# Another opening order, zeros written in 39 pieces, later q/k transposes and 42 matmuls of constants in a transformer layer

## The chip, the cores and the metric

One core of one Trainium2 chip runs the whole program. The metric is the device time of one execution in microseconds; the median of three executions of the kernel before is 1262.27 us.

## What is computed

One post-norm transformer layer over 2048 tokens of width 512. Of the reference, cut down:

```
qkv = x @ w_qkv                                  # 16 heads of 32
q, k = unit_norm(q), unit_norm(k)                # t * rsqrt(sum(t*t) + 1e-6)
q, k = rope on the even heads, unchanged on the odd ones
attn = softmax(causal(q @ k.T * q_gain))
x = layernorm(x + (attn @ v) @ w_out)
x = layernorm(x + routed_ffn(x) + shared_ffn(x)) # 8 experts, top 2, hidden 352; shared 704
```

## The kernel before

**Precision.** A product of float32 operands is made of three: each operand is split into a rounded high part and a low part, and high*high, low*high and high*low add up in PSUM. So each x tile is transposed by TensorE (PE), its high half is copied out by ScalarE (ACT, `xT_h`) and its low half by VectorE (DVE, `xT_l`).

**Attention.** Heads go in four groups of four (`g`), tokens in four chunks of 512 (`c`), 16 tiles of 128. For each group: 16 projections (`pe_project`, 12 matmuls of 384 columns, one tile each), whose q and k part ACT copies to `qk_even` or `qk_odd` and whose squares it writes to `squares`; `dve_norms` per chunk (a reduction, a chain of small operations, one large product, then the rotation of q, while GpSimd (POOL) rotates k); then q and k are turned (`pe_turn`, four transposes into `turn_ps`), split (`act_turn_high`, `dve_turn_low`), stored to DRAM and loaded again into `q_stack` and `k_stack` in another layout by the queue of SP (`stack`: two stores, a wait for both to land, three loads). Only then can the scores of that chunk begin.

**Slots.** A group's scores are 40 slots. Chunk 0 has slots 0 to 3, chunk 1 slots 4 to 11, chunk 2 slots 12 to 23, chunk 3 slots 24 to 39. In a slot PE makes the scores of one key tile, then whatever the tables put there, then the products with v of the slot before (`pe_values`); ACT takes the exponentials; the softmax sums are either matmuls on PE (slots in `DIRECT`) or additions on DVE (three heads) and POOL (one head), `key_sum`, which `pe_sums` gathers at the end of a chunk. Tables written by hand (`PROJECT_AT`, `NORMALISE_AT`, `TURN_AT`) say in which slot the projection, normalisation and turns stand; chunks 0 and 1 of the next group are prepared in slots 25 to 39 of this one. Each engine runs its own list strictly in this order, so what stands behind a waiting instruction waits too. Group 0 is written out, groups 1 and 2 are a loop, group 3 is written out again.

**Opening.** x comes through four buffers, so that a load waits for the transposes of the tile four before. All 16 tiles are transposed, chunks 0 and 1 of group 0 are projected, and one DMA writes 39 tiles of zeros (9984 KB) to `x_sorted`, which the expert stage needs much later.

**After attention** come the output projection, the router, the shared FFN and 39 expert tiles; the change touches there only the semaphore count that the scatter waits for.

Of the kernel before, what the change touches and what calls it, by code (L numbers as in the profile page):

```python
# [65 lines left out]
                (1, 0): 36, (1, 1): 37}  # L66
TURN_AT = {(2, 0): 8, (2, 1): 9,
           (3, 0): 15, (3, 1): 16,
           (0, 0): 31, (0, 1): 32,
           (1, 0): 38, (1, 1): 39}  # L70
# [8 lines left out]
NORM_AFTER = 7  # L79

FIRST_AFTER = 5
# [6 lines left out]
def work_at(table, slot, g):  # L88

    if table is TURN_AT and isinstance(g, int) and g == 0 and slot == 0:  # L90
        for which in range(2):
            yield 0, 1, which
# [12 lines left out]
def build(nc, x, w_qkv, w_out, q_gain, gate_w, w_gate, w_up, w_down, sw_gate, sw_up, sw_down,  # L105
          rope_cos, rope_sin, numbers, out):
    with ExitStack() as ctx:
# [21 lines left out]
        x_in = at("x_in", 135168, [P, 4, D], F32)  # L129
# [4 lines left out]
        squares = at("squares", 180224, [P, 2, TPC, HG, HD], F32)  # L134
        rope_prod = at("rope_prod", 180224, [P, 2, 4, TPC, HG // 2, HD // 2], F32)
# [35 lines left out]
        x_loaded = [sem(f"x_loaded{n}") for n in range(4)]  # L171
# [91 lines left out]
        zeros = at("zeros", 159744, [P, D], F32)  # L263
# [717 lines left out]
        def tail_gpsimd(pool):  # L981
# [11 lines left out]
            pool.wait_ge(zero_filled, 16)  # L993
# [54 lines left out]

        def load_w(sp, g):
# [6 lines left out]
        def _(sp):  # L1056
            for t in range(NT):
                if t >= 4:
                    sp.wait_ge(x_turned, t - 3)
                sp.dma_start(x_in[:, t % 4, :], x_rows[t * P:(t + 1) * P, :]).then_inc(x_loaded[t % 4], 16)  # L1060
                if t == 3:
                    load_w(sp, 0)
                    sp.dma_start(tile_numbers[:], numbers.rearrange("(a h) -> a h", a=1).broadcast_to([P, MAX_TILES])).then_inc(numbers_loaded, 16)
                    for to, of in ((cos, rope_cos), (sin, rope_sin)):
                        for c in range(NC):
                            sp.dma_start(to[:, c], of[c * CH:(c + 1) * CH, :].rearrange("(t p) f -> p t f", p=P)).then_inc(tables_loaded, 16)
                    sp.dma_start(gain[:], q_gain.rearrange("(a h) -> a h", a=1).broadcast_to([P, HEADS])).then_inc(tables_loaded, 16)
# [55 lines left out]
        def pe_project(g, c, tt):  # L1123
# [28 lines left out]
        def pe_scores(g, slot):  # L1152
# [7 lines left out]
            for p in range(2):  # L1160
                if later(g) or slot:
                    nc.tensor.wait_ge(exp_done, 2 * n + p - 1)
                for hh in range(2):
# [41 lines left out]
        def _(pe):  # L1205
            pe.wait_ge(consts_ready, 1)
            for t in range(NT):
                pe.wait_ge(x_loaded[t % 4], 16 * (t // 4 + 1))
                if t >= 4:
                    pe.wait_ge(xT_low, t - 3)  # L1210
                for k in range(KC):
                    mm = nc.tensor.transpose(scores[:, (t % 4) // 2, t % 2, k * P:(k + 1) * P],
                                             x_in[:, t % 4, k * P:(k + 1) * P], ident[:])
                mm.then_inc(x_turned, 1)
                if 0 <= t - FIRST_AFTER < TPC:

                    pe.wait_ge(xT_low, TPC)
                    pe.wait_ge(xT_high, TPC)
                    pe.wait_ge(ident_ready, 1)
                    pe_project(0, 0, t - FIRST_AFTER)  # L1220
            pe.wait_ge(xT_low, NT)
            pe.wait_ge(xT_high, NT)
            for which in range(2):
                pe_turn(0, 0, which)
            for tt in range(TPC):
                pe_project(0, 1, tt)
            def group(g):
                for slot in range(SLOTS):
# [3 lines left out]
                    for work in work_at(TURN_AT, slot, g):  # L1232
                        pe_turn(*work)
                    if slot or later(g):
# [5 lines left out]


        def act_copy_qkv(g, c, tt):
# [10 lines left out]
            if tt == 0 and (later(g) or c):  # L1253
                nc.scalar.wait_ge(q_roped, 2 * C)
                nc.scalar.wait_ge(k_roped, 2 * C)
            nc.scalar.activation(squares[:, :, tt], rows, ACT.Square)
# [296 lines left out]
```

## Time and profile before

| | us |
|---|---|
| median of 3 executions | 1262.27 (1262.16 to 1262.39) |
| the profiled execution | 1263.19 |
| its span | 1261.4 |
| TensorE busy in it | 1127.5 |

The sum of the prediction is made against the profiled execution's 1263.19 us, of which 1261.4 us are the span from the first to the last instruction and 1.8 us lie around it. Attention ends near 660 us of the span.

### The profile page before, as it was taken

What the parts mean: (1) busy time and instruction counts of PE and PEld (TensorE: products, weight loads), DVE (VectorE), ACT (ScalarE), POOL (GpSimd) and SP (SyncE); (2) the same over time, 40 slices, a digit from 0 to 9 for tenths busy, and PEclk for the clock granted to TensorE, in tenths of its full rate; (3) what the DMA queues carried; (4) which work ended last, traced back from release to release, by engine and by line L of the source; (5) the groups of instructions that cost most, each with busy time, mean ns of one, the idle gap of its engine ahead of it and who ended that gap; (6) DMA issues with size and microseconds to landing.
All of it is one profiled execution on the core that took longest, in us unless ns stands there. A gap on an engine that the chain in (4) does not pass through costs nothing.

```text
span 1261.4 us, 19831 instructions
## 1 busy us (share of the span) xinstructions
PE 1127.5 (89%) x6618; PEld 798.4 (63%) x6619; DVE 610.3 (48%) x1120; ACT 544.4 (43%) x894; POOL 499.9 (40%) x360
## 2 busy tenths in 40 slices
PE   5459899998979989998989999598999999999984
PEld 5446355654545545564337887367899999997763
DVE  2424876368553675645845846122222222222774
ACT  3226775566655666656852541011222332321131
POOL 1002555046340463422863206725246464622530
PEclk9869999999999999999988999789999999999997
DMA  5952502334131341324406302833244453412341
GB/s 144 367 148 70 139 11 84 101 84 117 51 101 44 84 125 43 101 59 125 144 1 207 117 1 85 310 105 92 95 143 153 135 166 127 146 59 76 107 160 67
DMA packets 90621, 141.73 MB, mean 112 GB/s; under 512 B 12272, under 2 KB 36848, under 8 KB 90544
## 3 DMA queue, kind: packets, MB, share of 16 engines
q1 hardware_dynamic: 74320, 103.48, 27.1%
q10 hardware_dynamic: 10944, 19.93, 4.6%
q0 software_dynamic: 5280, 17.31, 4.2%
q8 instruction: 47, 0.77, 0.3%
q14 instruction: 30, 0.25, 0.1%
HBM read 84.59 MB, written 56.10 MB: 112 GB/s over the span
## 4 chain that ended last, share of the span: by engine, by line
PE 64%; DVE 16%; issue 8%; POOL 4%; ACT 3%; DMA 2%; SPq 1%; another core or an unknown queue 1%; ACTq 0%; DVEq 0%; POOLq 0%
PE scores L497 12%; PE bank L1134 9%; PE scores L1166 7%; PE bank L490 7%; PE scores L554 5%; PE bank L1191 5%; PE bank L585 5%; PE scores L414 3%; PE bank L1188 3%; POOL key_sum L1493 3%; ACT probs L1292 2%; PE scores L512 1%; DVE key_sum L1407 1%; DVE x L861 1%; DMA turn_scratch<-turned_l 1%
## 5 line engine op out<-in xcount | busy, mean ns | idle before, releaser
L1292 ACT ACTIVATE probs<-scores,shift_now 128x1024 f32<-128x1024 f32 (+3 forms) x320 | 299.3, 985 | 132.8 <-PE scores L1166 62.5
L1166 PE MATMUL scores<-q_stack,k_stack 96*128 96x512 f32 (+3 forms) x640 | 205.7, 425 | 22.3 <-DMA k_stack<-turn_scratch 13.8
L1166 PEld LDWEIGHTS scores<-q_stack,k_stack 96*128 96x128 f32 x640 | 116.0, 198 | 155.3 <-issue 74.8
L1493 POOL TENSOR_TENSOR key_sum<-key_sum,probs 128x512 f32<-128x512 f32 (+2 forms) x76 | 154.4, 2031 | 128.1 <-ACT probs L1292 124.4
L1407 DVE TENSOR_TENSOR key_sum<-key_sum,probs 128x1536 f32<-128x1536 f32 (+2 forms) x76 | 157.0, 2066 | 42.7 <-ACT probs L1292 40.8
L1191 PE MATMUL bank<-probs,v_sb 128*32 128x512 f32 (+3 forms) x1280 | 152.4, 548 | 0.0
L497 PE MATMUL scores<-ffn_w,xt_h 128*128 x624 | 131.9, 334 | 4.6 <-issue 4.5
L964 POOL TENSOR_TENSOR ffn_w<-raw,ones 128x1408 fp32r<-128x1408 f32 (+2 forms) x36 | 71.6, 2000 | 150.7 <-PE bank L490 103.3
L554 PE MATMUL scores<-x1T_h,ffn_w 128*128 128x512 f32 (+1 forms) x384 | 104.2, 403 | 11.3 <-issue 8.9
L497 PEld LDWEIGHTS scores<-ffn_w,xt_h 128*128 128x128 f32 x624 | 103.4, 190 | 13.7 <-issue 11.7
L554 PEld LDWEIGHTS scores<-x1T_h,ffn_w 128*128 128x128 f32 (+1 forms) x384 | 69.1, 182 | 37.2 <-issue 13.5
L968 POOL TENSOR_TENSOR ffn_w<-raw,ffn_w 128x1408 fp32r<-128x1408 f32 (+2 forms) x36 | 90.6, 2527 | 2.1
L775 DVE TENSOR_TENSOR ht_l<-scores,ht_h 128x256 fp32r<-128x256 f32 x39 | 16.6, 425 | 146.7 <-ACT ht_h L649 146.7
L690 ACT CAST hid_h<-silu 128x512 fp32r<-128x512 f32 (+1 forms) x24 | 14.9, 620 | 149.9 <-DVE silu L806 130.6
L1381 POOL TENSOR_TENSOR rope_prod<-qk_even,cos 128x128 f32<-128x128 f32 x8 | 4.5, 564 | 187.5 <-DVE qk_even L1370 187.5
L490 PE MATMUL bank<-ffn_w,ht_h 128*128 (+1 forms) x234 | 70.4, 409 | 0.0
L1134 PE MATMUL bank<-wqkv_h,xT_h 128*128 128x384 f32 x256 | 60.3, 358 | 7.1 <-ACT v_sb L1260 7.1
L1191 PEld LDWEIGHTS bank<-probs,v_sb 128*32 128x32 f32 x1280 | 33.3, 111 | 50.6 <-issue 46.1
L1021 POOL DMA_INDIRECT extra<-y_sorted,place_int x32 | 35.3, 1102 | 71.7 <-DVE x L861 33.5
L497 PE MATMUL scores<-ffn_w,xt_l 128*128 x312 | 63.5, 325 | 0.0
L1188 PE MATMUL bank<-probs,ones 128*32 128x512 f32 (+3 forms) x576 | 62.7, 507 | 0.2
L585 PE MATMUL bank<-ffn_w,hid_h 128*128 128x512 f32 (+1 forms) x192 | 54.6, 413 | 8.6 <-ACT hid_h L690 7.1
(207 smaller groups left out, 1835.5 us busy)
## 6 DMA issues: line engine op xcount, KB each, us to landing
q_stack<-turn_scratch SPq DMA_DIRECT2D x48, 256.0 KB, 3.9
k_stack<-turn_scratch SPq DMA_DIRECT2D x48, 256.0 KB, 3.9
x_sorted<-zeros SPq DMA_DIRECT2D x1, 9984.0 KB, 28.9
y_sorted<-y_tile ACTq DMA_DIRECT2D x39, 256.0 KB, 2.2
x_tile<-x_sorted ACTq DMA_DIRECT2D x37, 256.0 KB, 2.7
turn_scratch<-turned_h SPq DMA_DIRECT2D x32, 256.0 KB, 2.9
turn_scratch<-turned_l SPq DMA_DIRECT2D x32, 256.0 KB, 3.1
raw<-w_gate SPq DMA_DIRECT2D x8, 704.0 KB
```

Of the source, the lines that this page charges most:

```text
L490: mm = nc.tensor.matmul(out_tile[:], hs[0:kn, k, :], moving(slot_before, DOWN + (low * 3 + k) * D, D, kn), start=(m == 0 and k == 0), stop ...
L497: mm = nc.tensor.matmul(to[:, 0:FH], xs[:, k, :], moving(slot, first + (low * KC + k) * FH, FH), start=(m == 0 and k == 0), stop=(m == 2 a ...
L554: mm = nc.tensor.matmul(scores[0:hn, which, n % 2, :], stationary(slot, at_, low, k, h0, hn), xs[:, k, c * CH:(c + 1) * CH], start=(m == 0 ...
L585: mm = nc.tensor.matmul(bank[n % 2][:], hs[0:kn, k, tt * P:(tt + 1) * P], ffn_w[0:kn, slot, first:first + D], start=(m == 0 and k == 0), s ...
L968: last = nc.gpsimd.tensor_tensor(low, src, high.bitcast(F32), ALU.subtract)
L1134: mm = nc.tensor.matmul(qkv_ps[:, 0:3 * P], xs[:, k, tok], ws[:, k, :], start=(m == 0 and k == 0), stop=(m == 2 and k == KC - 1))
L1166: mm = nc.tensor.matmul(scores[:, p, hh, lo:CH], k_stack[0:3 * HD, h, j * P:(j + 1) * P], q_stack[0:3 * HD, i % 2, h, lo:CH], start=True, ...
L1188: nc.tensor.matmul(sums_ps[HD * h:HD * (h + 1), lo:CH], ones[:], probs[:, slot % 4, h, lo:CH], start=first, stop=(j == last))
L1191: mm = nc.tensor.matmul(y_ps[HD * h:HD * (h + 1), lo:CH], v_sb[:, j, HD * h:HD * (h + 1)], probs[:, slot % 4, h, lo:CH], start=(j == 0), s ...
L1292: nc.scalar.activation(probs[:, slot % 4, 2 * p:2 * p + 2, lo:CH], scores[:, p, :, lo:CH], ACT.Exp, bias=shift_now[:, p:p + 1]).then_inc(e ...
L1407: nc.vector.tensor_tensor(key_sum[:, 0:3, lo:CH], key_sum[:, 0:3, lo:CH], probs[:, slot % 4, 0:3, lo:CH], ALU.add).then_inc(sum_dve, 1)
L1493: nc.gpsimd.tensor_tensor(key_sum[:, 3, lo:CH], key_sum[:, 3, lo:CH], new, ALU.add).then_inc(sum_pool, 1)
```

## The change

It has six parts. (1) x gets a buffer for each tile (`x_early` for 12, `x_late` for 4), SP issues all loads at once, w_qkv right after the first tile, the rope tables as two DMAs at the end. (2) The opening runs in the order of `OPENING`, the first projection right behind the first tile; DVE splits w after tile 0, and POOL's half of that split no longer waits for the tables. Tiles 12 to 15 are transposed in slots 4 to 6 of group 0, through the one bank `turn_ps`. (3) The zeros come from a source of 128x128, as 39 DMAs of 256 KB, 13 in each of groups 0 to 2. (4) `TURN_AT` is later everywhere: chunk 1's turns go to slots 0 and 2 of the group that uses them (in group 0: 2 and 3), chunk 0's from slots 31 and 32 to 33 and 36. The projections of chunk 1 go to slots 31 to 34, its normalisation to 35. (5) `DIRECT` loses slots 14, 15, 28, 29 and gains 13, 22. (6) 14 and 28 matmuls of bf16 ones stand ahead of and behind the first tile's transposes.

```
-              (1, 0): 32, (1, 1): 32, (1, 2): 34, (1, 3): 35}
+              (1, 0): 31, (1, 1): 32, (1, 2): 33, (1, 3): 34}
-                (1, 0): 36, (1, 1): 37}
-TURN_AT = {(2, 0): 8, (2, 1): 9,
+                (1, 0): 35, (1, 1): 36}
+TURN_AT = {(1, 0): 0, (1, 1): 2,
...
-DIRECT = set(range(STEP_AT[1])) | {4, 5, 6, 10, 11, 14, 15, 23, 28, 29, 30, 36, 38, 39}
+DIRECT = set(range(STEP_AT[1])) | {4, 5, 6, 10, 11, 13, 22, 23, 30, 36, 38, 39}
...
+FIRST_TURN_AT = (2, 3)
+EARLY = 3 * TPC
+LATE_X_AT = {4: [12], 5: [13, 14], 6: [15]}
+OPENING = [("x", 0), ("p", 0), ("x", 1), ("x", 2), ("p", 1), ("x", 3), ("x", 4), ("p", 2), ("x", 5), ("x", 6),
+           ("p", 3), ("x", 7), ("x", 8), ("p", 4), ("x", 9), ("p", 5), ("x", 10), ("p", 6), ("t", 0), ("t", 1),
+           ("x", 11), ("p", 7)]
+IDLE_MATMULS = (14, 28)
+FILL_AT = [4, 5, 6, 7, 11, 14, 15, 16, 25, 26, 27, 28, 29]
...
+                    if g < NG - 1 and slot in FILL_AT:
+                        sp.wait_ge(scores_ready, 2 * (SLOTS * g + slot))
+                        fill_zeros(len(FILL_AT) * g + FILL_AT.index(slot))
...
-                        sp.wait_ge(turned, 2 * (4 * g + 4))
+                        sp.wait_ge(turned, 2 * (NC * g + 3))
+                        sp.wait_ge(q_roped, 2 * (NC * g + 4))
+                        sp.wait_ge(k_roped, 2 * (NC * g + 4))
...
+        def pe_warm(count):
+            for _ in range(count):
+                nc.tensor.matmul(sums_ps[:, 0:P], ones_b[:], ones_b[:], start=True, stop=True)
...
+        def pe_turn_x(t):
+            nc.tensor.wait_ge(x_loaded[t], 16)
+            if t == EARLY:
+                nc.tensor.wait_ge(turn_low, 4)
+            elif t > EARLY:
+                nc.tensor.wait_ge(xT_low, t)
...
```

PE's list at the start of the program. Before, six x tiles (24 transposes) stand ahead of the first projection:

```order
L1212 MATMUL scores<-ident,x_in 128x128 x24
L1134 MATMUL bank<-wqkv_h,xT_h 128x384 x4
L1134 MATMUL bank<-wqkv_h,xT_l 128x384 x4
L1134 MATMUL bank<-wqkv_l,xT_h 128x384 x4
L1212 MATMUL scores<-ident,x_in 128x128 x4
```

And of the change, the same place:

```order
L1166 MATMUL bank<-ones_b 128x128 x14
L1178 MATMUL scores<-ident,x_early 128x128 x4
L1166 MATMUL bank<-ones_b 128x128 x28
L1159 MATMUL bank<-wqkv_h,xT_h 128x384 x4
L1159 MATMUL bank<-wqkv_h,xT_l 128x384 x4
L1159 MATMUL bank<-wqkv_l,xT_h 128x384 x4
L1178 MATMUL scores<-ident,x_early 128x128 x8
```

One tile stands ahead of the first projection, two behind it, and the constants' matmuls around the tile.

DVE's list at the end of group 0, slots 36 to 39 before (from the large product of chunk 1's normalisation on; `key_sum` 3x384 is slot 37, `turned_l` x2 are chunk 1's halves of slots 38 and 39):

```order
L1370 TENSOR_TENSOR qk_odd<-qk_odd,inv_norm 128x1024
L1381 TENSOR_TENSOR rope_prod<-qk_odd,cos 128x128
L1382 TENSOR_TENSOR rope_prod<-qk_odd,sin 128x128
L1383 TENSOR_TENSOR rope_prod<-qk_odd,sin 128x128
L1384 TENSOR_TENSOR rope_prod<-qk_odd,cos 128x128
L1386 TENSOR_TENSOR qk_odd<-rope_prod 128x8x16
L1387 TENSOR_TENSOR qk_odd<-rope_prod 128x8x16
L1407 TENSOR_TENSOR key_sum<-key_sum,probs 128x3x384
L1392 TENSOR_TENSOR turned_l<-bank,turned_h 128x512 x2
```

And of the change, slots 35 to 39, from the same product on:

```order
L1424 TENSOR_TENSOR qk_odd<-qk_odd,inv_norm 128x1024
L1435 TENSOR_TENSOR rope_prod<-qk_odd,cos 128x128
L1436 TENSOR_TENSOR rope_prod<-qk_odd,sin 128x128
L1437 TENSOR_TENSOR rope_prod<-qk_odd,sin 128x128
L1438 TENSOR_TENSOR rope_prod<-qk_odd,cos 128x128
L1440 TENSOR_TENSOR qk_odd<-rope_prod 128x8x16
L1441 TENSOR_TENSOR qk_odd<-rope_prod 128x8x16
L1446 TENSOR_TENSOR turned_l<-bank,turned_h 128x512
L1461 TENSOR_TENSOR key_sum<-key_sum,probs 128x3x384
```

The `turned_l` here is k of chunk 0 of the next group, turned in slot 36; before, it stood ahead of this normalisation (slot 32), and now it stands behind it.

PE's list around slots 4 to 6 of group 0 in the change (late x tiles into a bank that is not of `scores`):

```order
L1178 MATMUL bank<-ident,x_late 128x128 x4
L1235 MATMUL bank<-probs,ones 32x128 x4
L1238 MATMUL bank<-probs,v_sb 32x128 x4
L1213 MATMUL scores<-q_stack,k_stack 128x512 x4
L1178 MATMUL bank<-ident,x_late 128x128 x8
L1235 MATMUL bank<-probs,ones 32x512 x4
L1238 MATMUL bank<-probs,v_sb 32x512 x4
```

Two tiles (x8) stand in one slot, ahead of that slot's products with v; before, the slots held only scores and these products.

## Rows read from the trace of the kernel before

**Rows 1.** The page: busy us by engine; ACT's exponentials (busy, mean ns | idle before, releaser).
```profile
PE 1127.5 (89%) x6618; PEld 798.4 (63%) x6619; DVE 610.3 (48%) x1120; ACT 544.4 (43%) x894; POOL 499.9 (40%) x360
...
L1292 ACT ACTIVATE probs<-scores,shift_now 128x1024 f32<-128x1024 f32 (+3 forms) x320 | 299.3, 985 | 132.8 <-PE scores L1166 62.5
```

**Rows 2.** Timeline of the opening: start, duration in us, engine, line, operation [idle before <-releaser].
```profile
9.19 0.96 DVE L1333 CAST wqkv_h<-wqkv_raw 128x1536 fp32r<-128x1536 f32 x1 [0.18 <-DMA wqkv_raw<-w_qkv]
...
11.12 20.43 SPq L1060 DMA_DIRECT2D x_in<-x  x12
13.98 3.44 POOL L1475 TENSOR_TENSOR wqkv_l<-wqkv_raw,wqkv_h 128x1536 fp32r<-128x1536 f32 x1 [10.74 <-DMA gain<-q_gain]
14.91 1.97 PE L1212 MATMUL scores<-ident,x_in 128*128 128x128 f32 x8 [7.24 <-DMA x_in<-x]
...
22.96 0.60 PE L1212 MATMUL scores<-ident,x_in 128*128 128x128 f32 x4
...
30.68 1.22 DVE L1358 TENSOR_REDUCE sq_sum<-squares 128x32 f32<-128x1024 f32 x1 [4.58 <-ACT v_sb L1260]
31.59 0.43 SPq L1070 DMA_DIRECT2D x_sorted<-zeros  x1
...
38.15 0.28 DVE L1387 TENSOR_TENSOR qk_even<-rope_prod 128x128 f32<-128x128 f32 x1
...
42.74 0.59 ACT L1299 CAST xT_h<-scores 128x512 fp32r<-128x512 f32 x1
```

**Rows 3.** Chain that ended last, opening to the first scores: start, us, what.
```profile
24.12 2.34 PE bank L1134 x12
...
52.40 9.38 DMA turn_scratch<-turned_l
...
61.80 0.32 SPq L1089
...
74.07 0.76 PE scores L1166
```

**Rows 4.** DMA issues of the page: tensors, queue, count, KB each, us to landing.
```profile
x_sorted<-zeros SPq DMA_DIRECT2D x1, 9984.0 KB, 28.9
```

**Rows 5.** Windows, TensorE alone, start of group 2: stretch, its length, busy (x), PEclk, DMA share, GB/s.
```profile
374.00:382.00 8.00, 3.92 (x16) 0.50 0.53 156
```

**Rows 6.** The chain, slots 4 to 7 of group 0.
```profile
95.83 1.13 PE scores L1166 x4
...
100.78 0.99 PE bank L1188 x8
...
105.69 1.12 PE scores L1166 x4
```

**Rows 7.** The chain of group 1, and the start of group 2.
```profile
225.06 0.43 PE scores L1166
...
273.11 1.23 DVE sq_sum L1358
...
287.64 0.69 DVE turned_l L1392
...
292.41 0.68 PE scores L1166 x2
...
310.92 3.48 POOL wqkv_l L1475
...
359.27 1.22 DVE sq_sum L1358
...
369.18 0.65 DVE turned_l L1392
...
372.00 2.93 DMA q_stack<-turn_scratch
374.97 0.79 PE scores L1166
```

**Rows 8.** Waits of TensorE, whole attention: who for whom, us in total, times, longest.
```profile
PE bank L1148 <- DVE qk_odd L1387: 10.2, 7, 1.9
```

More of the change, by code:

```diff
@@ L88, in work_at @@
 def work_at(table, slot, g):
-    if table is TURN_AT and isinstance(g, int) and g == 0 and slot == 0:
-        for which in range(2):
-            yield 0, 1, which
+    if table is TURN_AT and isinstance(g, int) and g == 0 and slot < TPC:
+        if slot in FIRST_TURN_AT:
+            yield 0, 1, FIRST_TURN_AT.index(slot)
+        return
     for (c, part), at in table.items():
@@ L170, in build @@
         shift_steps, shift_copied = sem("shift_steps"), sem("shift_copied")
[L171 removed]
+        x_loaded = [sem(f"x_loaded{n}") for n in range(NT)]
         x_turned, xT_high, xT_low = sem("x_turned"), sem("xT_high"), sem("xT_low")
@@ L1136, in pe_project @@
             mm.then_inc(qkv_done, 1)
+        def pe_warm(count):
[7 more added lines that the diff above has]
+                nc.tensor.wait_ge(xT_low, t)
+            elif t >= 4:
+                nc.tensor.wait_ge(xT_low, t - 3)
+            for k in range(KC):
+                mm = nc.tensor.transpose(xT_bank(t)[:, k * P:(k + 1) * P], x_tile_in(t)[:, k * P:(k + 1) * P], ident[:])
+            mm.then_inc(x_turned, 1)
         def pe_turn(g, c, which):
             C = NC * g + c
+            if not later(g) and c == 2:
+                nc.tensor.wait_ge(xT_low, NT)
             if which == 0:
@@ L1205, in _ @@
         def _(pe):
+            pe.wait_ge(mask_filled, 1)
+            pe_warm(IDLE_MATMULS[0])
             pe.wait_ge(consts_ready, 1)
[L1207 to L1226, printed above, removed]
+            for kind, n in OPENING:
+                if (kind, n) == ("p", 0):
+                    pe_warm(IDLE_MATMULS[1])
+                if kind == "x":
+                    pe_turn_x(n)
+                elif kind == "p":
+                    pe_project(0, n // TPC, n % TPC)
+                else:
+                    pe_turn(0, 0, n)
             def group(g):
@@ L1233, in group @@
                         pe_turn(*work)
+                    if not later(g):
+                        for t in LATE_X_AT.get(slot, []):
+                            pe_turn_x(t)
                     if slot or later(g):
@@ L1239, in _, with squares_of, act_x_high @@
             tail_tensor(pe)
+        def squares_of(g, c):
+            return squares_second if not later(g) and c == 1 else squares
+        def act_x_high(t):
+            nc.scalar.wait_ge(x_turned, t + 1)
+            nc.scalar.copy(xT_h[:, :, t * P:(t + 1) * P], xT_bank(t).rearrange("p (k n) -> p k n", k=KC)).then_inc(xT_high, 1)
         def act_copy_qkv(g, c, tt):
@@ L1252, in act_copy_qkv @@
             nc.scalar.copy(qk[c % 2][:, :, tt], rows)
-            if tt == 0 and (later(g) or c):
+            if tt == 0 and (later(g) or c >= 2):
                 nc.scalar.wait_ge(q_roped, 2 * C)
                 nc.scalar.wait_ge(k_roped, 2 * C)
-            nc.scalar.activation(squares[:, :, tt], rows, ACT.Square)
+            nc.scalar.activation(squares_of(g, c)[:, :, tt], rows, ACT.Square)
             if later(g):
@@ L1279, in act_exp @@
             lo = max(0, (j - TPC * i) * P)
-            if not later(g) and slot == 3:
-                nc.scalar.wait_ge(zero_filled, 16)
             if not later(g) and slot == 0:
-                nc.scalar.wait_ge(x_turned, NT)
+                nc.scalar.wait_ge(x_turned, EARLY)
             if later(g) or slot >= 4:
@@ L1322, in group @@
                         act_turn_high(*work)
+                    if not later(g):
+                        for t in LATE_X_AT.get(slot, []):
+                            act_x_high(t)
             each_group(act, group)
@@ L1450, in _ @@
-            for which in range(2):
-                dve_turn_low(0, 0, which)
+            for t in range(8):
+                dve_x_low(t)
+                if t == 0:
+                    dve_split_w(0)
+            dve.wait_ge(tables_loaded, 16 * (3))
+            nc.vector.tensor_scalar(gain_abs[:], gain[:], -1.0, None, ALU.mult).then_inc(shift_steps, 1)
+            dve.wait_ge(shift_steps, 1)
+            nc.vector.tensor_tensor(gain_abs[:], gain_abs[:], gain[:], ALU.max).then_inc(shift_steps, 1)
@@ L1452, in _ @@
+            dve_norms(0, 0)
+            for t in range(8, EARLY):
+                dve_x_low(t)
+                if EARLY - 3 <= t < EARLY - 1:
+                    dve_turn_low(0, 0, t - EARLY + 3)
             dve_norms(0, 1)
@@ L1456, in group @@
                         dve_turn_low(*work)
+                    if not later(g):
+                        for t in LATE_X_AT.get(slot, []):
+                            dve_x_low(t)
                     if slot in STEP_AT and (slot or later(g)):
@@ L1486, in pool_add_keys @@
                 nc.gpsimd.wait_ge(sum_pool, added(g, slot) - 1)
+            if not later(g) and slot == first_added(ADDING[0]):
+                nc.gpsimd.wait_ge(x_turned, NT)
             if slot == first_added(i) and (later(g) or i > ADDING[0]):
```

105 lines of the change are left out of this document (53 added, 52 removed).

## Prediction

> **What bounds the kernel now.** I read the page first: TensorE (PE) is busy for 1127.5 of 1261.4 us [rows 1], so it is the engine to follow, and only stretches in which it waits, or does work that can go, are worth anything. Then the timeline of the opening: SP's loads of x are issued only from 11.12 us on; PE's next transposes begin at 14.91 after 7.24 us of waiting for x; POOL's half of the w split begins at 13.98, after the last table. The reader should see that DVE's first normalisation starts at 30.68 and that the DMA of zeros is issued at 31.59, just ahead of the first q/k stores [rows 2]. The chain shows what that does: the low half's store takes 9.38 us to land, the q loads start at 61.80, and the first scores come at 74.07 [rows 3]. From there I read the chain slot by slot in group 0 [rows 6] and group 1 [rows 7]: PE paces most slots, and hands over to DVE or POOL behind each normalisation and at the w split. The windows show a third limit: after a wait the clock stands at 1.2 GHz (PEclk 0.50) for 8 us and more, in which PE gets less done [rows 5].
>
> **The opening: 21 us gained.** w is now second in the queue instead of fifth and waits for no table. Four tiles and w, 1.8 MB, were in at 9.19 [rows 2], some 7 us after the first data; tile 0 and w are 1.05 MB, so my estimate is 6.5 us. DVE then rounds it (1 us), POOL subtracts (3.44 us [rows 2]): both halves by 11.0. The first projection ends at 11.8. The next must wait for ACT's copies (1.0) and for two halves of tile 1 (0.6 and 0.7): it ends at 16.8. After that a cycle is two tiles' transposes (0.60 each [rows 2]) and a projection (2.34 [rows 3]), about 3.65 us with the wait: the fourth ends at 24.1. DVE's tile 7 is out at 26.6, five small operations follow, and the normalisation starts at 27.7 against 30.68: only 3 us of the 6 saved on w arrive here, since a cycle now holds two tiles of x, and the normalisation stands behind tile 7. It takes 7.7 us as before (30.68 to 38.43 [rows 2]) and ends at 35.4. Then x tiles 8 and 9 and the q half on DVE, until 37.5; its store lands near 41 with nothing before it, where the wait lasted until 61.80. From the first q load to the first scores it was 12.3 us (61.80 to 74.07 [rows 3]): now 53.3. The gain is 21 us. If the tables, now last in the queue, come late or the landings are slow, 15; if the k half overlaps better, 24.
>
> The 42 constants' matmuls cost nothing by this: 28 of them at 0.11 to 0.15 us (a 128x128 transpose, four in 0.60 [rows 2]) are 3 to 4.2 us, from 4.8 to 9 at the latest, under the wait for w's low half at 11.0. Without that cover they would cost up to 4 us. They may keep the clock up for the first projection, which is also hidden.
>
> **Group 0, slots 0 to 7: 9 us lost.** Before, slot 4 began 21.8 us after slot 0 (95.83 less 74.07 [rows 3, 6]). Chunk 1's turns leave slot 0, but q is now turned in slot 2, 14.4 us in, and needs ACT and DVE (1.4), a store (3), three loads (1.3) and their landing (3 to 4): ready 23.5 to 24.5 us in. PE would be there at 20.3. So slot 4 comes about 2 us later than before relative to slot 0. In slots 4 to 6, the single bank makes the late x tiles a ping-pong: tile 13 waits for tile 12's two halves, which on ACT stand behind the exponentials, a copy of y and the copies of a projection; tile 14 in the same slot waits for two exponentials (0.985 each by the mean [rows 1], 1.06 of this width), ACT's 0.59 [rows 2] and DVE's 0.7 of tile 13. PE, counted through, reaches slot 7 16.5 us after slot 4 instead of 9.9 (95.83 to 105.69 [rows 6]): 1.8 us are the four tiles' transposes, 4.9 the two waits. Together 9 us; bounds 5 (q arrives in time, one wait hidden) and 13 (the clock falls as well).
>
> **Slots 8 to 25, each group: 2.7 us gained.** All times from here are on group 1's clock of the trace, as if its slot 0 began where it did. Today k and q of chunk 3 are turned in slots 15 and 16, where PE waits for the normalisation of 273.11 and then for DVE's half at 287.64, so that slot 17 starts only at 292.41 [rows 7]. With q at slot 18 and k at 22 these waits go. But slot 13 is now a direct one, the first to use the sums bank, and DVE reads the old sums only behind the normalisation, at 283.9; PE waits there for 2.5 us instead. Counting ACT's two exponentials a slot (2.1 us) and 2.4 us for an addition on DVE or POOL from there, slot 24 begins 3.8 us earlier. The w load now comes after q's stack in slot 18, some 3 us later than before, so w's low half, at 310.92 + 3.48 [rows 7], moves only to 311.8, and 2.7 us are left.
>
> **Slots 26 to 39 and the next group's start.** Two direct slots less are 2 x 0.99 us of PE (one direct slot's sums [rows 6]), the late turns take away PE's waits for q in slots 31 and 38 (seven such waits for the odd chunks alone are 10.2 us, the longest 1.9 [rows 8]); PE is done at 363.5 instead of just before 372.00 [rows 7]. But the scores of the next group need k of chunk 0, and its low half now stands on DVE behind chunk 1's normalisation. That begins at 356.8 (before 359.27 [rows 7]), takes 8.2 us, and the half is out at 365.7. From there to q's loads it was 2.2 us and their landing 2.93 (369.83, 372.00 [rows 7]); with three issues 6.5: scores at 372.2. So PE waits 8.7 us, and most of what it saved is given back. Against 374.97 [rows 7] this is 2.8 us better in group 1, whose end had a stall at the loop's turn already; groups 0 and 2 have none there, and for them the same sum gives 0.5 and 0.9 us. Moreover such a wait is as long as the one that brought the clock to 1.2 GHz before slot 0 of group 2 (0.50 from 374 to 382 [rows 5]); that costs slots 0 and 1 about 3 us in groups 1 and 3, while group 2 may even gain 1. Group 3 has no next group and keeps 2.5 of its gain: behind the w_out split POOL's two more additions take the rest.
>
> The 39 pieces of zeros: 9984 KB took 28.9 us [rows 4], so 0.74 us each, and they are spread over slots without a stack beside them; SP issues one in 0.43 [rows 2]. I count nothing. A piece that runs into a stack's store delays it by 0.74 at most, and PE only in slot 4 and at a group's end, where none stands. Beside it, the Trainium skill (DMA: Bandwidth & Descriptors, Rules for kernel authors) asks for at least 1 MiB a transfer, which speaks against the pieces; no trace here shows a 256 KB one of zeros, and rival (c) is what it would come to if they didn't hide.
>
> **Sum:** -21 + 9 - 0.5 - 2.8 - 0.9 - 2.5 + 6 - 1 = -13.7. The profiled execution would go from 1263.2 to 1249.5, the median, 0.9 lower today, to 1248.5.
>
> **Rivals.** (a) *The boundary's wait is shorter*: the normalisation starts or the landing ends 3 us sooner than counted at each of three boundaries, and the clock falls at one of them less: -9 and -3, 1236.5. For it: the start at 356.8 is counted through ten slots. Against it: k's half stands behind the normalisation in DVE's list. 0.25. (b) *The opening gives less*: x, which is issued at once, and 64-byte table pieces fill the queue, so that the first normalisation stays near 30.7; then only the zeros' removal counts, 15 us, and slots 4 to 6 cost 13: 1258. 0.14. (c) *Slower than before*: the zeros' pieces do not hide. SP's queue is one, and every store and load of a stack stands behind the pieces; 13.7/39 = 0.35 us of PE for each of the 39 would use up the gain; at 0.74 each it is -13.7 + 28.9 = +15.2, 1277.5. It decides from 0.35 us a piece on. Speaking for it: the 9.38 us landing beside the zeros [rows 3]. Against it: that was behind 10 MB, not 256 KB, and the slots were chosen between stacks. 0.06. (d) *The change does little*: the opening's gain is all taken back at boundaries at half clock (10 instead of 3 us each): within 2.5 us of 1262. 0.05.
>
> **How the numbers follow.** My forecast has 0.50: 1243 to 1255. The range reaches over (a) and (b): 1236 to 1259. A measurement of this kernel tells 0.2%, 2.5 us. Faster by more 0.92, the same 0.03, slower 0.05.
>
> **What would show it.** First scores at 53 us (51 to 59); POOL's split of w done by 11; the first normalisation at 27.7; slot 4 to slot 7 of group 0 16.5 us; PE waiting for k_stack's DMA before slot 0 of groups 1 to 3 for over 5 us, with PEclk 0.50; slots 15 and 16 without waits for turns. The prediction is wrong if PE runs through the group's boundary, or if the first normalisation doesn't move.

## The result and the profile after

The changed kernel is slower. Its median is 1268.9 us (1267.5 to 1269.7, four executions) against 1262.2 us of the kernel before, measured beside it; the ratio is 1.0051 with a 95% interval of 1.0032 to 1.0069. The forecast was 1248.5 us. The profiled execution took 1268.5 us, 5.3 more than that of before.

The page of the changed kernel: its span, and busy time by engine.

```profile
span 1266.6 us, 19869 instructions
...
PE 1129.4 (89%) x6596; PEld 804.2 (63%) x6597; DVE 623.7 (49%) x1128; ACT 541.2 (43%) x894; POOL 540.5 (43%) x368
```

TensorE has 22 instructions less than before, 64 of its sums matmuls having gone and 42 of constants come, and is busy 1.9 us longer [rows 1]. POOL is busy 40.6 us more with 8 instructions more. Both are signs to follow: matmuls at a lower clock, and work that got slower beside other work.

The chain of the changed kernel from the first load to the first scores: start, us, what.

```profile
2.27 5.12 DMA wqkv_raw<-w_qkv
...
8.46 3.46 POOL wqkv_l L1529
...
36.73 2.02 DMA turn_scratch<-turned_l
38.77 0.32 SPq L1106
...
50.72 0.77 PE scores L1213
```

The opening did what it should. The low half's store lands after 2.02 us where it took 9.38, and the scores come 23.35 us earlier than at 74.07 [rows 3]. So the loss lies behind 50.72, and there it is 28.6 us. To find it, the span is cut where a slot's first scores matmul starts. The table is worked out from those starts in the trace (us, rounded; "24 to 32" includes slot 32; the columns from the third on are sums over the groups named):

| kernel | to first scores | g0 slots 0 to 7 | g1 to g3 slots 0 to 7 | all slots 8 to 23 | g0 to g2 slots 24 to 32 | g0 to g2 slot 33 to next group | g3 slots 24 to 39 | rest |
|---|---|---|---|---|---|---|---|---|
| before | 74.1 | 36.6 | 102.1 | 200.4 | 120.8 | 77.4 | 45.0 | 604.9 |
| after | 50.7 | 47.4 | 107.2 | 199.2 | 121.7 | 88.6 | 45.6 | 606.2 |
| e1, whole loop as before | 51.5 | 47.4 | 98.9 | 200.6 | 121.9 | 74.1 | 45.3 | 602.8 |
| e12, only DIRECT new | 50.2 | 47.6 | 99.0 | 200.4 | 136.1 | 76.8 | 46.3 | 605.5 |
| e7, only DIRECT old | 51.8 | 47.2 | 106.7 | 190.2 | 109.6 | 89.2 | 44.9 | 605.5 |
| e9, 28 and 29 direct again | 52.2 | 47.1 | 107.0 | 194.2 | 107.4 | 89.2 | 43.6 | 608.0 |
| e3, k half in slot 34 | 50.5 | 48.9 | 104.8 | 198.9 | 122.6 | 66.6 | 46.8 | 602.9 |
| e10, e7 and e3 together | 50.6 | 47.4 | 105.2 | 187.7 | 109.3 | 66.7 | 44.1 | 604.9 |
| e11, e10 with both x edits | 52.1 | 35.0 | 104.9 | 188.1 | 109.7 | 66.9 | 43.6 | 608.3 |

Against before, the changed kernel loses 10.7 in group 0's slots 0 to 7, 5.2 in the others', and 11.2 from slot 33 to the next group. What should have paid for it, the slots 8 to 32, gives 0.4. The waits say where TensorE stands now. The view of waits, changed kernel: who for whom, us in total, times, longest.

```profile
PE scores L1213 <- DMA k_stack<-turn_scratch: 16.8, 2, 8.7
PE bank L1159 <- ACT v_sb L1309: 14.4, 5, 4.6
PE bank L1235 <- DVE inv_sum L1470: 11.7, 4, 3.0
...
PE bank L1178 <- DVE xT_l L1380: 3.5, 2, 1.9
```

Each line is one place. The first is the group's boundary, the second slot 32, the third slot 14 (four groups, 3 us each), the last the late x tiles. The view puts the third boundary's 8.2 us down to "issue" instead of k. The boundary's wait stood in the forecast at its size, slot 14's at 2.5, the late x waits at 4.9 in all; the wait in slot 32 did not stand there.

**Slot 14.** The timeline of group 1 around it, rows of DVE and PE: start, duration, engine, line, operation [idle before].

```profile
273.67 1.22 DVE L1424 TENSOR_TENSOR qk_odd<-qk_odd,inv_norm 128x1024 f32<-128x1024 f32 x1
...
277.18 0.70 DVE L1470 STREAM_TRANSPOSE inv_sum<-bank 128x512 f32<-128x512 f32 x1
...
278.03 1.93 PE L1235 MATMUL bank<-probs,ones 128*32 128x512 f32 x8 [2.96 <-DVE inv_sum L1470]
...
279.71 1.96 PE L1238 MATMUL bank<-probs,v_sb 128*32 128x512 f32 x8
...
281.60 2.08 PE L1213 MATMUL scores<-q_stack,k_stack 96*128 96x512 f32 x4
```

The windows of the same place, TensorE alone: stretch, length, busy (x), PEclk, DMA share, GB/s.

```profile
274.00:278.00 4.00, 1.07 (x4) 0.85 0.00 0
278.00:282.00 4.00, 3.97 (x17) 0.50 0.35 125
```

Slot 13 is a direct one now, its sums go to the bank that DVE still has to read, and DVE reads it only behind the normalisation. TensorE waits 2.96 us, and then sums, products and scores run at half clock (0.50 in the window 278.00:282.00), 1.93, 1.96 and 2.08 us, where at full clock they are 1.07, 1.07 and 1.20 (e7's rows below). The wait was forecast at 2.5; that the work behind it doubles was not.

**Slot 32.** The timeline of group 1, slots 29 to 32, DVE, POOL, ACT and PE:

```profile
326.22 1.76 DVE L1461 TENSOR_TENSOR key_sum<-key_sum,probs 128x1536 f32<-128x1536 f32 x1 [2.48 <-ACT probs L1341]
327.90 1.21 DVE L1412 TENSOR_REDUCE sq_sum<-squares 128x32 f32<-128x1024 f32 x1
...
336.01 1.97 POOL L1441 TENSOR_TENSOR qk_even<-rope_prod 128x128 f32<-128x128 f32 x1
...
338.07 0.38 ACT L1305 ACTIVATE squares<-bank 128x256 f32<-128x256 f32 x1 [6.53 <-POOL qk_even L1441]
...
338.66 1.65 PE L1159 MATMUL bank<-wqkv_h,xT_h 128*128 128x384 f32 x4 [4.55 <-ACT v_sb L1309]
340.11 1.48 PE L1159 MATMUL bank<-wqkv_h,xT_l 128*128 128x384 f32 x4
```

The addition of slot 29 stands on DVE ahead of chunk 0's normalisation and waits for that slot's exponentials. So the reduction starts at 327.90, the rotation of k ends on POOL at 337.98, and only then may ACT write `squares` of chunk 1's first projection (both use the same memory). The last product of that rotation took 1.97 us here, beside DVE's next addition, and 0.45 in e9 below. TensorE, which needs the projection's bank again, waits 4.55 us, and again works at half clock behind it: 1.65 and 1.48 us for four matmuls that take 0.86 to 0.97 at full clock.

**The boundary.** The chain from group 1 to group 2:

```profile
356.88 1.22 DVE sq_sum L1412
...
364.56 0.69 DVE turned_l L1446
365.26 2.04 DMA turn_scratch<-turned_l
...
368.21 4.74 DMA k_stack<-turn_scratch
...
373.19 0.79 PE scores L1213
```

This is the forecast's chain, link for link: the low half of k behind the normalisation, two landings, scores. A trap lies in it: the normalisation was forecast at 356.8 "on group 1's clock of the trace" and starts at 356.88, but group 1 itself began at 217.7 and not 225.06 [rows 7]. Within the group it is 7.4 us late. The windows behind the three boundaries:

```profile
217.00:225.00 8.00, 7.29 (x47) 0.68 0.00 0
373.00:381.00 8.00, 7.81 (x46) 0.61 0.00 0
528.00:536.00 8.00, 7.25 (x39) 0.50 0.01 2
```

Each group now starts below full clock; before, groups 1 and 3 started at 1.00 (windows 225.00:233.00 and 528.00:536.00) and only group 2 at 0.50 [rows 5].

### The profile page after: what moved, and what is told of

Its sections match the earlier page's. It is cut to its first block, busy times and chain, and to the rows that moved or that the text cites. A ratio compares the mean times of both kernels' runs of the same rounds, so it can differ in the third digit from the quotient of the medians.

```text
span 1266.6 us, 19869 instructions
## 1 busy us (share of the span) xinstructions
PE 1129.4 (89%) x6596; PEld 804.2 (63%) x6597; DVE 623.7 (49%) x1128; ACT 541.2 (43%) x894; POOL 540.5 (43%) x368
## 4 chain that ended last, share of the span: by engine, by line
PE 66%; DVE 13%; issue 8%; POOL 5%; ACT 3%; DMA 2%; another core or an unknown queue 1%; SPq 0%; ACTq 0%; POOLq 0%; DVEq 0%
PE scores L505 12%; PE bank L1159 10%; PE scores L1213 9%; PE bank L1238 7%; PE bank L498 6%; PE scores L562 6%; PE bank L593 5%; PE scores L422 3%; PE bank L1235 3%; ACT probs L1341 2%; POOL key_sum L1549 2%; DVE x L869 2%; PE scores L520 1%; PE scores L1216 1%
## 5 line engine op out<-in xcount | busy, mean ns | idle before, releaser
L1213 PE MATMUL scores<-q_stack,k_stack 96*128 96x512 f32 (+3 forms) x640 | 208.6, 429 | 48.0 <-issue 18.9
L1549 POOL TENSOR_TENSOR key_sum<-key_sum,probs 128x512 f32<-128x512 f32 (+1 forms) x84 | 190.5, 2268 | 88.6 <-ACT probs L1341 84.2
L1461 DVE TENSOR_TENSOR key_sum<-key_sum,probs 128x1536 f32<-128x1536 f32 (+1 forms) x84 | 179.5, 2137 | 68.9 <-ACT probs L1341 66.9
L1446 DVE TENSOR_TENSOR turned_l<-bank,turned_h 128x512 fp32r<-128x512 f32 x32 | 21.9, 686 | 110.0 <-ACT turned_h L1316 109.9
L1235 PE MATMUL bank<-probs,ones 128*32 128x512 f32 (+3 forms) x512 | 53.9, 495 | 11.7 <-DVE inv_sum L1470 11.7
L1238 PEld LDWEIGHTS bank<-probs,v_sb 128*32 128x32 f32 x1280 | 32.8, 112 | 47.6 <-issue 41.2
```

The lines of the kernel that those rows point to most:

```text
L1213: mm = nc.tensor.matmul(scores[:, p, hh, lo:CH], k_stack[0:3 * HD, h, j * P:(j + 1) * P], q_stack[0:3 * HD, i % 2, h, lo:CH], start=True, ...
L1235: nc.tensor.matmul(sums_ps[HD * h:HD * (h + 1), lo:CH], ones[:], probs[:, slot % 4, h, lo:CH], start=first, stop=(j == last))
L1238: mm = nc.tensor.matmul(y_ps[HD * h:HD * (h + 1), lo:CH], v_sb[:, j, HD * h:HD * (h + 1)], probs[:, slot % 4, h, lo:CH], start=(j == 0), s ...
L1461: nc.vector.tensor_tensor(key_sum[:, 0:3, lo:CH], key_sum[:, 0:3, lo:CH], probs[:, slot % 4, 0:3, lo:CH], ALU.add).then_inc(sum_dve, 1)
L1549: nc.gpsimd.tensor_tensor(key_sum[:, 3, lo:CH], key_sum[:, 3, lo:CH], new, ALU.add).then_inc(sum_pool, 1)
```

## The experiments

All kernels have one of two bases, named with each. Ratios are against the kernel before, run beside them. Its medians were 1262.2 us beside the changed kernel, 1266.0 beside e1 to e4, 1263.5 beside e5 to e8 and 1265.6 beside e9 to e12, so a difference between kernels of two of these series is uncertain by some 4 us. Theory 1 is the one of the forecast's own parts (each part costs what its place shows, and they add up); the rival is in each expectation.

**e1: the whole loop as before, everything else new.**

```
-              (1, 0): 31, (1, 1): 32, (1, 2): 33, (1, 3): 34}
+              (1, 0): 32, (1, 1): 32, (1, 2): 34, (1, 3): 35}
...
-DIRECT = set(range(STEP_AT[1])) | {4, 5, 6, 10, 11, 13, 22, 23, 30, 36, 38, 39}
+DIRECT = set(range(STEP_AT[1])) | {4, 5, 6, 10, 11, 14, 15, 23, 28, 29, 30, 36, 38, 39}
```

(The other two tables likewise.)

> The change with the projection, normalisation and turn tables and the direct slots of before; opening order, late x tiles, chunk 1's first turns in slots 2 and 3, zeros in 39 pieces and the constants' matmuls stay. By stages of the trace of the change, the opening gains 23.4 us and slots 0 to 8 of group 0 lose 10.8. Theory 1 (the later turns and the other direct slots lose the rest, mostly at the groups' boundaries): all groups take from slot 8 on what they took before, so about 1262.2 - 23.4 + 10.8 = 1249.6, within 2. Rival 2 (the 39 pieces of zeros slow the groups they lie in, whatever the tables): groups 0 to 2 stay longer and the time is 1258 to 1268.

Measured: 1245.5 us, ratio 0.986 (0.980 to 0.991). That is 2 us below the range of theory 1 and far from the rival. The new opening, group 0's late x tiles included, is good for about 20 us, and the new loop takes 23 away.

**e2: the kernel before with the new tables and the new DIRECT** (and the waits of SP and the turns of group 0's chunk 1 that the new tables need).

> The kernel before with only the new tables, the new direct slots and the w load's waits that go with them; opening, x buffers and the single zeros DMA of before. Theory 1: it is slower by what the groups lost from slot 8 of group 0 on, 16 to 19 us: 1278 to 1281, with TensorE waiting for k_stack before slot 0 of groups 1 to 3. Rival 2 (the zeros' pieces are what slows the groups): 1260 to 1266.

Measured: 1282.1 us, ratio 1.012 (1.009 to 1.015), 1 us above theory 1's range. The loss is the loop's own; it needs neither the early opening nor the zeros' pieces. Its table, cut the same way, has 107.1 us in groups 1 to 3's slots 0 to 7, 122.8 in the slots 24 to 32 and 88.8 from slot 33 on, as the changed kernel.

**e3: the k half of chunk 0 turned two slots earlier.**

```
-           (0, 0): 33, (0, 1): 36}
+           (0, 0): 33, (0, 1): 34}
```

> The change with one number other: k of chunk 0 of the next group is turned in slot 34 instead of 36, so that its low half stands on VectorE ahead of chunk 1's normalisation, not behind it. Theory 1 (this half behind the normalisation makes TensorE wait 5.6 to 10 us at each of three boundaries, and the clock falls to 1.2 GHz after it): the waits go, 5 us at each boundary and 3 us of slow clock at two of them: 1268.9 - 21 = 1248, at least 12 us less. Rival 3 (what ends last at the boundary is the normalisation of chunk 1 itself, through the additions and the sums of chunk 3): only 0 to 5 us less, 1264 to 1269.

Measured: 1245.5 us, ratio 0.983 (0.980 to 0.986), theory 1. One number gives 23 us. Its slots 33 to the next group are 66.6 us in sum, 10.8 less than even before.

**e4: the four late x tiles turned in the opening.**

```
-LATE_X_AT = {4: [12], 5: [13, 14], 6: [15]}
+LATE_X_AT = {}
...
-           ("x", 11), ("p", 7)]
+           ("x", 11), ("p", 7), ("x", 12), ("x", 13), ("x", 14), ("x", 15)]
```

> The change with x tiles 12 to 15 transposed behind the last projection of the opening, where TensorE waits for the first k anyway, instead of in slots 4 to 6 of group 0. Theory 1 (the single bank's ping-pong and its waits cost 6 to 8 us there, and TensorE's idle stretch before the first scores is free): 1261 to 1263. Rival 4 (VectorE's four halves delay chunk 1's normalisation, so that q comes later to slot 4, and the gain goes): 1266 to 1269.

Measured: 1262.7 us, ratio 0.997 (0.995 to 0.999), theory 1. The slots 4 to 7 of group 0 took 16.4 us and not 24.2, and the first scores still came at 50.2: in the opening the four tiles cost nothing, since TensorE waits there for q's way through DRAM.

**e5: no matmuls of constants.**

```
-IDLE_MATMULS = (14, 28)
+IDLE_MATMULS = (0, 0)
```

> The change without the 42 matmuls of constants. Theory 1 (the first projection waits 1.86 us for w's low half anyway, so neither their time nor the clock they keep up is on the path): the first scores within 1 us of 50.7, the whole within 0.15% of the change (1267 to 1271). Rival 5 (without them the first transposes and projections run at 1.2 GHz): first scores 1.5 to 3 us later, 1270 to 1272.

Measured: 1267.0 us, ratio 1.0020 (1.0000 to 1.0041), whose interval overlaps that of the changed kernel. The timeline shows why; the first projection of e5:

```profile
8.15 1.65 PE L1159 MATMUL bank<-wqkv_h,xT_h 128*128 128x384 f32 x4 [3.53 <-DVE wqkv_h L1387]
...
9.60 1.48 PE L1159 MATMUL bank<-wqkv_h,xT_l 128*128 128x384 f32 x4
11.69 0.97 PE L1159 MATMUL bank<-wqkv_l,xT_h 128*128 128x384 f32 x4 [0.61 <-POOL wqkv_l L1529]
```

Without the constants the first two sets take 1.65 and 1.48 us, as in slot 32 at half clock (the view's clock reads 1.00 here, so this rests on the durations), but they end before POOL's half of w is there. The scores began at 50.5 against 50.7.

**e6: all 39 pieces of zeros issued in the opening,** ahead of the first store, in the slots none.

> The change with all 39 pieces of zeros issued right behind the loads, ahead of the first q/k stores, instead of spread over slots. Theory 1 (the opening's gain is mostly the store of q and k that no longer stands behind 10 MB of zeros): the pieces run from about 20 to 50 us, the low half of q lands near 50 instead of 38.8, first scores at 60 to 63: 10 to 12 us slower than the change, 1279 to 1281. Rival 6 (the gain is the earlier projections; 39 pieces from 20 us on are nearly over when the stores come at 36): first scores at 51 to 54, 1269 to 1272.

Measured: 1291.3 us, ratio 1.021 (1.016 to 1.026), 22 more than the changed kernel and 10 more than expected. The first scores came at 70.1, 19.4 later. SP's queue in e6:

```profile
19.43 34.90 SPq L1085 DMA_DIRECT2D x_sorted<-zeros  x39
54.37 0.86 SPq L1097 DMA_DIRECT2D turn_scratch<-turned_h  x1
```

The pieces went out over 34.90 us, and q's store stands behind them on the same queue; the one large DMA landed in 28.9 [rows 4] after a single issue of 0.43 [rows 2]. In the slots the same pieces cost nothing that shows: the loop of e6, which has none of them, is no shorter than the changed kernel's (613.5 us from the first scores to the last slot of group 3, against 609.7). The Trainium skill (DMA: Bandwidth & Descriptors, Rules for kernel authors), cited in the forecast against pieces below 1 MiB, agrees in direction with e6. That the size is the reason is not shown, since the pieces also come from a narrower source, 512 bytes a row where it had 2048. Spread over the slots it doesn't matter.

**e7: only DIRECT as before** (14, 15, 28, 29 direct, 13 and 22 not).

> The change with the direct slots of before (14, 15, 28, 29 back, 13, 22 out), the later turns kept. Theory 1 (the additions of slots 28 and 29 delay chunk 0's normalisation, by which TensorE waits 4.5 us in slot 32 of groups 0 to 2, and stand behind the w_out split on GpSimd in group 3, 7.5 us instead of 3.2; slot 13 as a direct one costs 2.8 us of waiting in each group): those go and two more direct slots cost 2 us a group, 1256 to 1263. Rival 7 (TensorE's work counts more than these waits): 1269 to 1277.

Measured: 1242.3 us, ratio 0.981 (0.977 to 0.986): 26.6 us less than the changed kernel, where 6 to 13 were expected. It is a cost of the size of the k turn's (which of the two is the larger isn't shown: their intervals overlap), and I had not seen it. The table says where: -9.0 in the slots 8 to 23 and -12.1 in the slots 24 to 32. Slot 14 in e7, DVE and PE:

```profile
273.41 0.70 DVE L1470 STREAM_TRANSPOSE inv_sum<-bank 128x512 f32<-128x512 f32 x1
...
274.26 1.07 PE L1235 MATMUL bank<-probs,ones 128*32 128x512 f32 x8 [1.09 <-DVE inv_sum L1470]
...
275.12 1.07 PE L1238 MATMUL bank<-probs,v_sb 128*32 128x512 f32 x8
...
276.12 1.20 PE L1213 MATMUL scores<-q_stack,k_stack 96*128 96x512 f32 x4
```

The direct slots 14 and 15 come a slot later, the wait is 1.09 and the clock stays up.

**e8: e1 with the late x tiles in the opening and group 0's chunk 1 turned in slots 0 and 1.**

```
-FIRST_TURN_AT = (2, 3)
+FIRST_TURN_AT = (0, 1)
```

> Opening order, zeros in pieces and constants of the change; projection, normalisation and turn tables and direct slots of before; x tiles 12 to 15 transposed in the opening; chunk 1's first turns in slots 0 and 1 of group 0 instead of 2 and 3. Theory 1 (terms add: run e1 less the ping-pong's 7.8 us and the 3 us wait for q in slot 4): 1233 to 1236. Rival 8 (chunk 1's normalisation isn't done by slot 0, so the turns make TensorE wait there): 1238 to 1242.

Measured: 1234.5 us, ratio 0.976 (0.971 to 0.981). The parts of the opening and of group 0 add up: its slots 0 to 7 took 35.0 us, 1.6 less than before.

**e9: slots 28 and 29 direct again, 13 and 22 kept.**

```
-DIRECT = set(range(STEP_AT[1])) | {4, 5, 6, 10, 11, 13, 22, 23, 30, 36, 38, 39}
+DIRECT = set(range(STEP_AT[1])) | {4, 5, 6, 10, 11, 13, 22, 23, 28, 29, 30, 36, 38, 39}
```

> The changed kernel with one edit: the slots 28 and 29 accumulate on TensorE again (DIRECT holds them as before), while 13 and 22 stay in the place of 14 and 15. Theory 1: what DIRECT costs comes for the most part from these two slots, whose additions on GpSimd delay the squares and norm of the next group's chunk 0 behind them. In the kernel with DIRECT as before, slot 32 took 4.2 us and not 10.4 to 11.3, the slots 24 to 31 took 32.0 to 32.7 us and not 29.3 to 29.7, and in the last group 24.7 and not 27.1. That gives -6.8 x 3 + 2.8 x 3 - 2.4 = -14.4, so 1268.9 - 14.4 = about 1254.5 (1252 to 1257), with the slots 8 to 23 still at about 49.6 us a group. Theory 2: the swap of 14 and 15 for 13 and 22 carries the cost: at least 1263, and slot 32 keeps its wait.

Measured: 1249.7 us, ratio 0.988 (0.984 to 0.991): 19.2 us less, theory 1, by more than it said. Slot 29 and 32 of group 1 in e9, DVE, POOL, ACT and PE:

```profile
317.03 1.22 DVE L1412 TENSOR_REDUCE sq_sum<-squares 128x32 f32<-128x1024 f32 x1 [4.13 <-ACT v_sb L1309]
...
325.20 0.45 POOL L1441 TENSOR_TENSOR qk_even<-rope_prod 128x128 f32<-128x128 f32 x1
...
326.14 0.39 ACT L1305 ACTIVATE squares<-bank 128x256 f32<-128x256 f32 x1
...
328.65 0.86 PE L1159 MATMUL bank<-wqkv_h,xT_h 128*128 128x384 f32 x4
```

Slot 29 begins at 316.6 here and at 323.2 in the changed kernel. The reduction starts 0.4 us into it instead of 4.7, the rotation ends before ACT wants the memory, and TensorE doesn't wait; slot 32 took 4.2 us in each group, where it was 10.4 to 11.3. Of e7's 26.6 us, 7.4 are left for the swap of 14 and 15 for 13 and 22.

One part was not in the expectation: in the slots 8 to 23, whose DIRECT e9 shares with the changed kernel, groups 0 to 2 took 48.0, 48.3 and 48.1 us, not 49.6, 50.4 and 49.5. At slot 14 of group 1, e9 waits 2.50 for `inv_sum` and the clock stays at full:

```profile
269.00:273.00 4.00, 1.76 (x12) 1.00 0.00 0
273.00:277.00 4.00, 3.74 (x28) 1.00 0.29 103
```

So the clock after this wait, full here and half in the changed kernel, carries some 1.6 us a group. In group 3 of e9 it fell (wait 2.44), and that group took 49.8 as in the changed kernel (49.7). This gain is not one of the edit for sure: e5 has the changed kernel's tables and DIRECT, and there the clock fell behind slot 14 in two groups and not in four, and the same slots took 195.6 us in sum instead of 199.2. The length of the wait does not settle it either. Slot 14 of group 2 in e4, whose clock fell (0.50 in the window 427.00:430.00), and of group 0 in e9, whose clock stayed:

```profile
426.45 1.86 PE L1231 MATMUL bank<-probs,ones 128*32 128x512 f32 x8 [1.86 <-DVE inv_sum L1466]
124.09 1.06 PE L1235 MATMUL bank<-probs,ones 128*32 128x512 f32 x8 [2.69 <-DVE inv_sum L1470]
```

Over the eight kernels with 13 as a direct slot, the granted clock of the 8 us from these sums on was below 1.00 behind 24 of the 32 waits: behind all 20 of 2.73 us and more, and behind four of the eight between 1.86 and 2.69. What decides among those stays open.

**e10: e7 and e3 together.**

> The changed kernel with DIRECT as before and the k half of the next group's chunk 0 turned in slot 34 and not 36. Each edit alone took away 23 to 27 us. Theory 1: they are two costs in two places: DIRECT in the slots 8 to 32, the k half in the slots 33 to the next group's start (29.3, 29.9, 29.4 us against 21.2, 24.3, 21.1, so -22.0). They add up: 1242.3 - 22 = about 1220 (1217 to 1223). Theory 2: both edits take away one and the same wait, the boundary's: the two together stay at 1238 to 1245.

Measured: 1218.4 us, ratio 0.964 (0.961 to 0.968). By the medians the two add up, 1268.9 - 26.6 - 23.4 = 1218.9; by the ratios less well, 1.0051 - 0.022 - 0.024 = 0.959 against 0.964. The table shows it more closely: e10 has e7's slots 8 to 32 to within 3 us (297.0 against 299.8) and e3's boundaries (66.7, 66.6). They are two waits in two places. The k half in e10, DVE and SP at the end of group 1:

```profile
329.66 0.69 DVE L1446 TENSOR_TENSOR turned_l<-bank,turned_h 128x512 fp32r<-128x512 f32 x1 [2.29 <-ACT turned_h L1316]
...
334.33 1.21 DVE L1412 TENSOR_REDUCE sq_sum<-squares 128x32 f32<-128x1024 f32 x1
```

```profile
335.30 1.27 SPq L1106 DMA_DIRECT2D k_stack<-turn_scratch  x3
```

The low half is out 4.0 us before the normalisation starts, the loads are issued 9.4 us before the next group's scores at 344.73, and TensorE doesn't wait for k. The 3.21 us that it stands idle there, in front of group 2, the view puts down to "issue", and e1 has 3.10 at the same place; the clock is 0.57 behind them.

**e11: e10 with the x edits of e8.**

> The kernel of the run before in this list with the four late x tiles turned in the opening and the first group's chunk 1 turned in the slots 0 and 1. Theory 1 (the slots 4 to 7 of the first group lose 7.8 to 8.8 us of waits, and the slots 0 to 3 some 3 us, as in the runs with these edits): 1220 - 8.3 - 3.5 = about 1208 (1205 to 1212). Theory 2 (the waits show again at the next place where chunk 0 or 1 is wanted): 1215 or more.

Measured: 1206.7 us, ratio 0.954 (0.950 to 0.957), the fastest kernel of this case, 27.8 us below e8, which has the tables of before. The later tables are worth having; what made the change slow was the one k turn, DIRECT, the late x and group 0's turns in slots 2 and 3. The page of e11:

```profile
PE 1118.0 (93%) x6660; PEld 801.0 (66%) x6661; DVE 603.9 (50%) x1120; ACT 541.0 (45%) x894; POOL 499.5 (41%) x360
```

TensorE makes 64 matmuls more than in the changed kernel and is busy 11.4 us less.

**e12: DIRECT of the change on the tables of before** (e1 and DIRECT).

> The changed kernel with the three tables of before and the DIRECT of the change, so that it differs from the run with the whole loop as before (1245.5) by DIRECT alone. Theory 1 (DIRECT costs by itself: the additions of 28 and 29 stand on GpSimd and VectorE ahead of the norm of chunk 0, which is turned two slots later): half to all of what it costs with the new tables, so 1252 to 1265, with a longer slot 31 or 32. Theory 2 (its cost needs the late turns of the tables): 1243 to 1248.

Measured: 1267.1 us, ratio 1.0016 (0.9991 to 1.0042), 21.6 us more than e1: DIRECT costs by itself, theory 1, and a little over its range. It shows at another place. Group 1, slot 31 of e12:

```profile
334.42 0.28 DVE L1441 TENSOR_TENSOR qk_even<-rope_prod 128x128 f32<-128x128 f32 x1
334.84 1.11 PE L1193 MATMUL bank<-ident,qk_even 128*128 128x128 f32 x4 [6.85 <-DVE qk_even L1441]
```

With q turned in slot 31 the late normalisation is waited for by the turn, 6.85 us, instead of by the projection in slot 32. The slots 24 to 32 are 136.1 us in sum against 121.9. The slots 8 to 23 don't change (200.4, 200.6), presumably since there the turns of slots 15 and 16 wait anyway.

## Why the prediction was wrong

It said -13.7; the span went +5.2. Taken by its own steps:

- **The opening, -21:** -23.35. Right, and a little small. POOL's split ended at 11.9 (forecast 11.0), the first normalisation started at 26.89 (27.7), the loads of q went out at 38.77 (near 41). e1 bears the gain out by itself.
- **Group 0, slots 0 to 7, +9:** +10.7. Right. q came late by 2.97 us in slot 3 and the two late tiles of slot 5 waited 1.50 and 1.79; e4 gave back 7.8 of it.
- **Constants, 0:** right (e5). **Zeros, 0:** right (e6's loop is no shorter without them). Rival (c), the only one on the slower side, did not occur.
- **"Slot 24 begins 3.8 us earlier": this is the step that failed.** -3.8 in each of four groups is -15.2; the slots 8 to 23 gave -1.2, so 14.0 of the 18.9 us of error lie here. The tables' part of it exists: with DIRECT of before the same turns gave -10.2 (e7) and -12.7 (e10). DIRECT took back 9.0 of it by e7, by the wait for `inv_sum`, which I had at 2.5 and which took 2.9, and by the half clock behind it, which I had left out (some 1.6 us a group). I had allowed for the clock at the boundaries alone, from [rows 5]. The half clock comes and goes: e5, with the same tables and DIRECT, has 195.6 us where the changed kernel has 199.2. The other 5.0 us of the miss (2.5 by e10) belong to the tables, whose gain I had too high; no run takes that part to pieces.
- **"Two direct slots less are 2 x 0.99 us of PE": the same mistake, a second time.** TensorE did save it: the slots 24 to 31 of group 1 took 29.7 us, and 31.5 in e9, which has the two direct slots back. But where the two additions go was not followed. They stand ahead of the normalisation of chunk 0, and slot 32 took 10.4 us where e9 has 4.2. I let the addition of slot 29 delay nothing. From slot 24 to the next group the change lost 4.8, 2.5 and 4.7 us, where my sums, less their 3.8, held +3.3, +1.0 and +2.9. With group 3 (+0.6 against +1.3) that is 4.1 us of the error.
- **The boundary, a wait for k behind the normalisation:** right as a mechanism, as the chain shows, and shown by e3. The length of 8.7 us is luck in part: the normalisation and TensorE both came some 7 to 8 us later within the group than forecast. What I did not work out is what the late k costs in all: e3 sets it at 23 us, as much as the opening gives.
- **The clock at the boundaries, +6 - 1:** the slots 0 to 7 of groups 1 to 3 lost 5.2, but this agreement is luck. In e3, whose groups 1 and 3 start at full clock, the slots 0 to 3 still took 19.5 and 19.6 us against 17.1 before: chunk 1's turns now stand in slots 0 and 2, and in group 1 the sums wait 1.41 for POOL there. I had put that at nothing. In the changed kernel these slots took 20.1 and 21.4, so the clock itself cost 0.6 and 1.9 where I had 3 each, and group 2 gained 2.1 and not 1.
- The rest: -2.4 and +1.7 from the first two points, +0.2 from the slots 0 to 7 of groups 1 to 3 and +1.2 behind attention, which no step claimed. With the 14.0 and the 4.1 that is 18.8, the 18.9 but for rounding.

The range had the lower side covered by mechanisms and its upper side by a smaller opening alone. A rival "DIRECT costs" was missing, though the diff has the line.

## What to carry to other kernels

Moving an addition from TensorE to another engine isn't finished with TensorE's saving: go down the other engine's list to the next thing that somebody waits for, here the normalisation, and price the delay there. Price a wait of TensorE with the matmuls that may follow at half clock, not by its length alone: here that was another 1.6 us. And a change of many parts that comes out at nothing can hold a good kernel: here four small corrections, found from TensorE's waits, turned +0.5% into -4.6%.

## What the hardware showed that I had not expected

- A wait of 2.96 us in the middle of full work was followed by a stretch at 0.50 (1.2 GHz), a wait of 2.50 us at the same slot of another kernel by one at 1.00 (2.4 GHz), and one of 1.86 us again by 0.50. The Trainium skill (TensorE: Matmul & The Clock Gate, HAM oscillation — how this bites in real kernels) says that a kernel which keeps waiting for data between bursts starts each burst cold. Slot 14 of every group and slot 32 of groups 0 to 2 of the changed kernel agree, with waits for DVE and ACT and not for a DMA.
- One addition on POOL, 128x512, took 1.26 to 1.28 us when DVE was not adding and up to 2.87 beside DVE's own addition. It goes the other way too: in e9 POOL's addition at 306.94 took 1.28, and DVE's, begun 0.07 us behind it, 2.83 instead of 1.76. The group of these additions, by its form, in the changed kernel: minimum, median, maximum in ns.

```profile
L1549 POOL TENSOR_TENSOR key_sum<-key_sum,probs x84: 1001/2616/2872, 101.3 to 658.0; 128x512 f32<-128x512 f32 x72, 128x384 f32<-128x384 f32 x12
```

- In group 3 the additions stand behind the w_out split in POOL's list, and the exponentials wait for one of them. The addition itself is not slow there, 1.23 us; the pieces of the split ahead of it are long (changed kernel, chain and ACT):

```profile
631.59 6.06 POOL wo_l L986
...
639.37 1.23 POOL key_sum L1549
...
640.75 2.12 ACT L1341 ACTIVATE probs<-scores,shift_now 128x1024 f32<-128x1024 f32 x2 [8.95 <-POOL key_sum L1549]
```

- 39 DMAs of 256 KB, written from one tile of 128x128, were issued over 34.90 us when nothing stood between them, where a single DMA of the same 9984 KB from a tile of 128x512 landed in 28.9.
